# Four layers in one program: new planned costs, attention-value products by batch, and maxima laid between attention units

## The chip, the cores and the metric

The kernel runs on one core of a Trainium2 chip. The metric is the device time of one execution in microseconds. The engines are TensorE (PE, with its weight loads as PEld), VectorE (DVE), ScalarE (ACT), GpSimd (POOL) and SyncE (SP), which issues most transfers.

## The reference

The input x has 8 batches of 256 positions and 128 features; everything is float32. Four layers follow each other, each with a residual.

```python
x = x + moe0(x, cond)      # 2 shared blocks silu(x w1) * (x w3) w2, 8 experts gelu(x W1e) W2e, top 2 of 8
x = x + moe1(x, cond)      # 4 such shared blocks, 8 experts, top 2 of 8
# layer 2: a recurrence over the 256 positions
def step(h, z_t):
    gate = sigmoid(h @ Wh.T + z_t @ Wz.T + b)
    return tanh(h * (1 - alpha) + gate * z_t)
x = x + scan(step, h_t=cond, z=x)
# layer 3: causal attention, 16 heads of 8, with one more key and value made from cond
scores = q @ k.T / sqrt(8); causal; softmax; out = attn @ v; out @ c_proj_w + c_proj_b
x = x + attention(x, cond)
```

## The kernel before, in words

Positions are cut into 8 chunks of 32 (256 columns with the 8 batches). Both expert layers run chunk by chunk. The recurrence follows one chunk behind: step t is a product on TensorE (STEP, L1200), a tanh on ScalarE (GATE, L956), a scan on VectorE (SCAN, L1529) and a tanh on ScalarE (NEW, L961), with one small product on GpSimd (DECAY, L772). Each step needs the one before. All other work is laid between the steps. Behind some steps TensorE gets filler matmuls (L1204), so many that the planned work up to the next step reaches `DENSE` (0.62 us).

Attention works on 4 tiles t of 64 queries (`QT`). For each tile:
- KP and QP (L1053) project keys and queries, K and Q (L1060) spread them by groups of heads; QZ makes four copies of the queries, each masked to one head of a group, on VectorE (L1429) or, where `QZ_ACT` says so, on ScalarE (L912). V (L1067) makes the values, in two units of four batches.
- A (L1084, L1088) makes scores with the queries as rows, and VectorE takes each row's maximum (L1443). There are 1, 2, 4 and 4 such units a batch for t = 0 to 3. L and MT turn the maxima of a pair of batches p, with the image key's scores, into rows; SyncE writes these into QZ's copies (`rows_in`), so that the later scores come out less their maximum.
- S (L1132) makes scores with the keys as rows, for a batch b, half of the heads gg and block of 128 keys kb. On the diagonal block the causal term is added: for tiles in `CAUSAL_PE` by a further product on TensorE (L1137), for the others by VectorE (SC, L1496), which also moves the scores to SBUF. ScalarE takes the exponential (L947) into one of 8 buffers `pt`.
- AV (L1156) multiplies them with the values: 8 products of 32 output rows (16 records in the trace, as f32 goes in two), each in one of four column groups of the array. AC (L935) copies the sums out, X (L1112, L1116) transposes them and adds the image value's share, VectorE divides (L1479, L1484), TR and O (L1125, L1162) transpose back and project.

Tiles 0 and 1 have keys, queries and maxima made while the last two chunks' steps run (`EARLY`). The rest follows after the recurrence.

Nobody writes the order down. `plan` lists units with what they need, and `schedule` simulates the engines with the durations of `costs`: among the units that could start within `EAGER` us of the earliest, it takes the one listed first. `fits` keeps a unit out of the room before the next step, unless it ends in time, within `SLACK`. The resulting four lists are the program's order on each engine. No duration is used in any other way, apart from the number of fillers (`warming`). TensorE writes results into 4 banks of PSUM, 6 once the recurrence is over.

Of the kernel before, what the change touches and what calls it, by code (L numbers as in the profile page):

```python
# [24 lines left out]
ALU = mybir.AluOpType  # L25
# [92 lines left out]
def costs(key):  # L118

    k, c = key[0], key[1] if len(key) > 1 else 0  # L120
    if k == "W":
        a, b = PIECES[key[2]][1:]
        return {"act": (.18 + (b - a) * .00085,), "dve": (.16 + (b - a) * .00104,)}
# [28 lines left out]

# [10 lines left out]
def schedule(units):  # L163
# [15 lines left out]
    for key in chain + [u[0] for u in units]:  # L179
        family = (key[:3] if key[0] in ("R", "SA", "SB", "E", "M", "GT") else key if key[0] == "Y" else  # L180
                  key[0] if key[0] in ("STEP", "GATE", "SCAN", "NEW", "DECAY") else "P" if key[0] in ("KP", "QP") else key[:2])
# [25 lines left out]
    def start(key, part, eng):  # L207
# [17 lines left out]
        if eng == "pe":  # L225
            if key in banked:
# [18 lines left out]
        if eng == "act":  # L245
# [7 lines left out]
            if kind == "S" and s_users.index(key) >= NPT:  # L253
                av = (("AV",) + s_users[s_users.index(key) - NPT][1:], "pe")
# [53 lines left out]
    while queues:  # L308
        found = []
        for (eng, family), queue in queues.items():  # L310
            key, part = queue[0]
            at = start(key, part, eng)
            if at is not None and fits(key, eng, at, costs(key)[eng][part]):
                found.append((at, eng, number[key], family))
# [7 lines left out]
        if eng == "pe":  # L322
# [1289 lines left out]
```

## Time and profile before

| | |
|---|---|
| median of 3 runs | 479.9 us (478.22 to 479.98) |
| span of the profiled execution | 478.1 us |
| its share outside the span, by the median run | 1.8 us |
| TensorE, VectorE, ScalarE busy | 442.8, 309.3, 261.2 us |
| recurrence, first to last gate | 43.6 to 342.5 us |

The page of the profile gives its own execution's span; that execution's time outside the profiler is not known, so the median run stands beside it. Busy times add up what an engine worked on, whatever it cost the whole. The rows come after the change.

### The profile page before, as it was taken

To read this page: it belongs to the slowest core of one execution; us is meant where nothing else is said; L and a number is where in the kernel's file an instruction comes from. 1 tells how busy PE (TensorE), PEld (TensorE's weight loads), DVE (VectorE), ACT (ScalarE), POOL (GpSimd) and SP (SyncE) were. 2 spreads that over 40 slices of the span, in tenths; PEclk is the share of its full clock that TensorE was granted. 3 is DMA by queue.
4 is the path that set the end of the run, shared out by engine and by line. 5 is a ranking of instruction groups with operands and counts; after the bars stand their busy time and mean duration, and the time that the engine had idled before them with its cause. 6 is when DMAs were issued, how large, how long until landed. Compare 5 with 4: busy or idle time off the path is not lost.

```text
span 478.1 us, 13039 instructions
## 1 busy us (share of the span) xinstructions
PE 442.8 (93%) x4530; PEld 310.0 (65%) x4530; DVE 309.3 (65%) x999; ACT 261.2 (55%) x885; POOL 85.9 (18%) x365
## 2 busy tenths in 40 slices
PE   3999999899999999999998998999998798999984
PEld 2787787667777777776756766566655464656652
DVE  6774666666656556656557665576449978569851
ACT  3552646545646556456474356654777159764461
POOL 7120313221413213213121121211100000000000
PEclk9999999999999999999999999999999999999995
DMA  8400000000000000000000000000000001001000
GB/s 314 149 12 8 6 0 1 3 0 1 3 0 2 2 2 1 1 2 1 1 1 4 1 1 2 1 3 2 2 4 22 2 2 23 6 3 26 2 4 22
DMA packets 11222, 7.70 MB, mean 16 GB/s; under 512 B 8983, under 2 KB 10263, under 8 KB 11159
## 3 DMA queue, kind: packets, MB, share of 16 engines
q1 hardware_dynamic: 10727, 6.61, 4.5%
q8 instruction: 38, 0.62, 0.5%
q10 hardware_dynamic: 432, 0.27, 0.2%
q14 instruction: 25, 0.20, 0.1%
HBM read 5.39 MB, written 1.05 MB: 13 GB/s over the span
## 4 chain that ended last, share of the span: by engine, by line
PE 70%; ACT 13%; DVE 11%; issue 4%; DMA 1%; POOL 0%; ACTq 0%; DVEq 0%
PE ybk L1035 17%; PE cbk L1200 11%; PE hid L1180 7%; PE ybk L1156 6%; DVE cbk L1529 4%; ACT dd L956 4%; ACT hb L882 3%; DVE wm L1443 3%; ACT hs L961 2%; PE hid L1132 2%; PE vbk L1180 2%; PE hid L1084 2%; PE hid L1060 2%; PE hid L1053 1%; PE hid L1021 1%
## 5 line engine op out<-in xcount | busy, mean ns | idle before, releaser
L1529 DVE TENSOR_TENSOR_SCAN cbk<-dd 128x24 f32<-128x24 f32 x256 | 55.7, 218 | 102.3 <-ACT dd L956 98.9
L1200 PEld LDWEIGHTS cbk<-hs,rec 128*128 128x128 f32 x512 | 76.4, 188 | 56.2 <-ACT hs L961 49.1
L1200 PE MATMUL cbk<-hs,rec 128*128 128x8 f32 x512 | 91.5, 251 | 7.7 <-ACT hs L961 3.7
L772 POOL TENSOR_TENSOR dd<-hs,leak 128x8 f32<-128x8 f32 x256 | 55.1, 215 | 233.0 <-ACT hs L961 230.4
L1035 PE MATMUL ybk<-hg,down 128*128 128x256 f32 x352 | 95.8, 398 | 0.5 <-DVE hg L1405 0.2
L961 ACT ACTIVATE hs<-cbk 128x8 f32<-128x8 f32 x256 | 45.3, 177 | 70.5 <-DVE cbk L1529 69.2
L956 ACT ACTIVATE dd<-cbk 128x8 f32<-128x8 f32 x256 | 46.4, 181 | 61.6 <-PE cbk L1200 60.1
L1180 PE MATMUL hid<-xsp,up 128*128 128x256 f16 x528 | 73.1, 277 | 2.4 <-ACT hb L882 0.6
L1035 PEld LDWEIGHTS ybk<-hg,down 128*128 128x128 f32 x352 | 60.7, 191 | 6.3 <-DVE hg L1405 0.9
L1180 PEld LDWEIGHTS hid<-xsp,up 128*128 128x128 f16 x528 | 49.7, 105 | 10.9 <-ACT hb L882 2.9
L1156 PE MATMUL ybk<-hb,vx 128*32 128x64 f32 (+1 forms) x1536 | 38.2, 223 | 2.5 <-ACT hb L947 1.9
L1156 PEld LDWEIGHTS ybk<-hb,vx 128*32 128x32 f32 (+1 forms) x1536 | 25.5, 108 | 18.4 <-ACT hb L947 9.2
L947 ACT ACTIVATE hb<-hb 128x512 f32<-128x512 f32 (+1 forms) x48 | 29.2, 622 | 11.7 <-DVE hb L1496 8.7
L1405 DVE TENSOR_TENSOR hg<-hb,hid 128x512 f32<-128x512 f32 x49 | 32.9, 676 | 2.9 <-PE hid L1021 2.8
L882 ACT ACTIVATE hb<-hid 128x512 f32<-128x512 f32 x54 | 32.0, 593 | 2.6 <-PE hid L1180 2.0
L1443 DVE TENSOR_REDUCE wm<-hid 128x2 f32<-128x384 f32 (+3 forms) x49 | 29.6, 617 | 1.2 <-PE hid L1088 1.0
L1204 PE MATMUL cbk<-id 128*128 128x256 f16 x143 | 23.3, 270 | 0.0
L1496 DVE TENSOR_TENSOR hb<-hid,later 128x512 f32<-128x512 f32 (+1 forms) x27 | 18.0, 680 | 5.8 <-PE hid L1132 5.8
L1084 PE MATMUL hid<-kp,qz 128*128 128x128 f16 (+3 forms) x140 | 17.8, 233 | 3.3 <-DVE wm L1443 1.8
L1180 PE MATMUL vbk<-xsp,up 128*128 128x256 f16 x144 | 20.3, 278 | 0.2
L1132 PE MATMUL hid<-qz,kp 128*128 128x256 f16 (+1 forms) x102 | 19.5, 279 | 0.2 <-DVE wm L1443 0.2
L1021 PE MATMUL hid<-gt,sel 128*128 128x256 f16 x98 | 17.7, 273 | 0.2
(231 smaller groups left out, 661.0 us busy)
## 6 DMA issues: line engine op xcount, KB each, us to landing
qz<-up_in SPq DMA_DIRECT2D x3, 512.0 KB, 6.8
out_dram<-silu SPq DMA_DIRECT2D x4, 256.0 KB, 2.9
x<-x_in SPq DMA_DIRECT2D x7, 128.0 KB, 8.2
down<-down_in SPq DMA_DIRECT2D x1, 768.0 KB, 8.6
att<-att_in SPq DMA_DIRECT2D x1, 743.0 KB, 9.4
down<-down_in SPq DMA_DIRECT2D x1, 640.0 KB, 6.2
kp<-mrow SPq DMA_DIRECT2D x32, 4.0 KB
qz<-rows SPq DMA_DIRECT2D x32, 2.0 KB, 1.7
```

What stands on the lines that cost most here:

```text
L772: tts(dd[:, t % ZR, 1, :, 2], hs[:, t, :], leak[:, 0:1].broadcast_to([P, B]), ALU.mult).then_inc(decay, 1)
L882: nc.scalar.activation(hb[:, i % NHB, :], hid[bank_of[key]][:], ACT.Gelu, scale=1 / WS).then_inc(act_done, 1)
L947: nc.scalar.activation(pt[0:ks, i % NPT, :], scores, ACT.Exp, scale=SC).then_inc(act_done, 1)
L956: nc.scalar.activation(dd[:, t % ZR, 1, :, 0], cbk[c % 2][:, o:o + B], ACT.Tanh, scale=0.5).then_inc(gate_th, 1)
L961: nc.scalar.activation(hs[:, t + 1, :], new, ACT.Tanh).then_inc(h_full, 1)
L1035: m = pe.matmul(ybk[l][:, 0:n], D(l, "w2" if shared else "e2", e * f + i), hg[:, hg_of[made] % NHG, i * n:i * n + n], start=first and i == ...
L1156: m = pe.matmul(abk[i % 2][HP * j:HP * j + HP, g * P + QT * (b % 2):g * P + QT * (b % 2) + QT], vx[0:ks, kb, at:at + HP], w[:, (r * J + j) ...
L1180: m = pe.matmul(into, up[:, pw, a:a + P], x_part(c, l, px, slice(0, n)), start=j == 0, stop=j == 2)
L1200: pe.matmul(cbk[c % 2][:, o:o + B], wh, hs[:, t, :], start=False, stop=True, skip_group_check=True).then_inc(gate_pre, 1)
L1405: i = tts(hg[:, hg_of[key] % NHG, w], hb[:, hb_of["E", c, l, e] % NHB, w], hk[:, w], ALU.mult)
L1443: i = nc.vector.tensor_reduce(wm[:, t % 2, b, a * n + r.start:a * n + r.stop], hk[:, r.start * nk:r.stop * nk].rearrange("p (h k) -> p h k ...
L1529: nc.vector.tensor_tensor_scan(vps[chunk_of(t) % 2], dd[:, t % ZR, 0].rearrange("p b o -> p (b o)"), dd[:, t % ZR, 1].rearrange("p b o -> ...
```

## The change

- `costs` gets other durations, many of them shorter, and `schedule` counts a tail after a unit's end for each engine (`tail`) and a switch of the array's shape on TensorE (`switch`: 0.165 us into a narrower shape, 0.08 us out of it). `EAGER` goes from 0.1 to 0.03. At most two A units wait for VectorE (`MOST_A`). S, SC and AV each form one queue over all tiles.
- AV is one unit a batch: all 16 or 32 (for t = 2, 3) products with their second records follow each other.
- V is one unit a tile: four batches go to rows 0 to 63 of the bank, four to rows 64 to 127, alternating.
- `CAUSAL_PE` is (0, 1, 2): the addition on VectorE stays for t = 3 alone.
- `QZ_ACT` is empty: all of QZ is VectorE's.
- The maxima of a tile are listed between the attention units of the tile before, pair by pair; keys and queries of t = 3 come after the last pair of t = 1 (`KQ3 = 3`).

```diff
-QZ_ACT = ((), (), (0, 1, 2, 3), (0, 1, 2, 3))
+QZ_ACT = ((), (), (), ())
-EAGER = .1
+EAGER = .03
+MOST_A = 2
+KQ3 = 3
+INTO, OUT_OF = .165, .08
-CAUSAL_PE = (0,)
+CAUSAL_PE = (0, 1, 2)
...
     if k == "A":
-        return {"pe": ((.66, .38, .23, .28)[c],), "dve": (.69 if c != 2 else .55,)}
+        return {"pe": ((.66, .34, .23, .275)[c],), "dve": (.6 if c != 2 else .47,)}
     if k == "S":
-        return {"pe": (.43 if key[4] == c // 2 and not diagonal(key) else .22,), "act": (.6,)}
+        return {"pe": (.43 if key[4] == c // 2 and not diagonal(key) else .22,), "act": (.5,)}
     if k == "SC":
-        return {"dve": (.69,)}
+        return {"dve": (.6,)}
+    if k == "AV":
+        return {"pe": (.446 * (c // 2 + 1) + (INTO if c == 2 else 0),)}
...
-        "GT": {"pe": (.21,), "act": (.37,)}, "SA": {"pe": (.65,), "act": (.59,), "dve": (.69,)},
-        "SB": {"pe": (.65,), "dve": (.69,)}, "E": {"pe": (.65,), "act": (.59,)}, "M": {"pe": (.22,), "dve": (.69,)},
+        "GT": {"pe": (.13,), "act": (.27,)}, "SA": {"pe": (.655,), "act": (.5,), "dve": (.61,)},
+        "SB": {"pe": (.655,), "dve": (.61,)}, "E": {"pe": (.655,), "act": (.5,)}, "M": {"pe": (.22,), "dve": (.6,)},
...
-        "V": {"pe": (.48,), "dve": (.69,)}, "L": {"dve": (.2,)}, "MT": {"pe": (.55,), "act": (.25,), "dve": (.45,)},
-        "EI": {"act": (.25,)}, "AV": {"pe": (.4,)}, "AC": {"act": (.6,)}, "X": {"pe": (.85,), "dve": (.26, .29)},
+        "V": {"pe": (.44,), "dve": (.56, .56)}, "L": {"dve": (.15,)}, "MT": {"pe": (.25,), "act": (.17,), "dve": (.4,)},
+        "EI": {"act": (.2,)}, "AC": {"act": (.5,)}, "X": {"pe": (.84,), "dve": (.23, .24)},
...
+    tail = {"pe": .17, "act": .1, "dve": .08, "pool": 0.0}
...
+            if kind == "A" and sum(1 for k in users if k and k[0] == "A" and (k, "dve") not in end) >= MOST_A:
+                return None
...
+    def switch(key):
+
+        of = tiling(key)
+        if of == shape[0]:
+            return 0.0
+        return INTO if of != (P, P) else OUT_OF
...
+            if at is not None and eng == "pe" and not part and number[key] >= 0:
+                at = max(at, free["pe"] + switch(key))
...
-            end[key, eng] = free[eng] + (.17 if eng == "pe" else 0)
+            end[key, eng] = free[eng] + (tail[eng] if number[key] >= 0 or eng == "pe" else 0)
...
-    attend(0)
+    attend(0, *range(B // 2))
     keys_and_queries(2)
     for p in range(B // 2):
         maxima(2, p)
-    attend(1)
-    keys_and_queries(3)
-    maxima(3, 0)
-    attend(2)
-    attend(3, 1)
+        attend(1, p)
+        if p == KQ3:
+            keys_and_queries(3)
+    for p in range(B // 2):
+        maxima(3, p)
+        attend(2, p)
+    attend(3, *range(B // 2))
...
                 elif kind == "V":
-                    _, t, q = key
-                    r = slice(QT * (t % 2), QT * (t % 2) + QT)
+
+                    _, t = key
                     pe.wait_ge(dve_done, nth["dve", ("X3", t * QT + XP)])
                     for i in range(4):
-                        m = pe.matmul(hk[r, i * P:i * P + P], x3[:, 4 * q + i, t * QT:(t + 1) * QT], A("wv"),
-                                      start=True, stop=True)
+                        for q in range(2):
+                            m = pe.matmul(hk[QT * q:QT * q + QT, i * P:i * P + P], x3[:, 4 * q + i, t * QT:(t + 1) * QT],
+                                          A("wv"), start=True, stop=True)
...
+                    for kb in range(t // 2 + 1):
+                        ks = keys_of(t, kb)
+                        for gg in range(2):
+                            pe.wait_ge(act_done, nth["act", ("S", t, b, gg, kb)])
+                            w = pt[0:ks, s_order["S", t, b, gg, kb] % NPT, :]
```

## Rows read from the trace of the kernel before

**Rows 1.** The page, the span in 40 equal slices, in tenths

```profile
PE   3999999899999999999998998999998798999984
...
PEclk9999999999999999999999999999999999999995
```

**Rows 2.** The gate's line: durations in ns, first and last start

```profile
L956 ACT ACTIVATE dd<-cbk x256: 163/182/184, 43.6 to 342.5; 128x8 f32<-128x8 f32 x128
```

**Rows 3.** Timeline, three places in the recurrence: start, us, engine, line

```profile
271.46 0.31 PE L1200 MATMUL cbk<-hs,rec 128*128 128x8 f32 x2
...
272.58 0.31 PE L1200 MATMUL cbk<-hs,rec 128*128 128x8 f32 x2
...
291.20 1.28 ACT L927 ACT_TABLE_LOAD   x1
```

**Rows 4.** Stretches: length, busy us of PE, PEld, DVE, ACT, POOL, granted clock

```profile
43.00:342.00 299.00, 287.81 (x2263) 211.46 (x2261) 185.84 (x698) 163.45 (x695) 71.77 (x332) 1.00 0.01 2
342.00:359.00 17.00, 16.91 (x237) 9.80 (x236) 7.09 (x17) 13.20 (x26) 0.20 (x1) 1.00 0.04 10
359.00:385.00 26.00, 21.64 (x303) 12.79 (x302) 25.12 (x62) 11.55 (x25) 0.00 (x0) 1.00 0.04 8
...
434.00:455.00 21.00, 20.16 (x380) 12.82 (x378) 18.94 (x39) 10.55 (x22) 0.00 (x0) 1.00 0.07 16
455.00:466.00 11.00, 9.11 (x233) 5.59 (x231) 6.10 (x12) 8.05 (x17) 0.00 (x0) 1.00 0.02 5
```

**Rows 5.** Timeline: two operations of a kind in a row, VectorE and ScalarE

```profile
343.49 1.14 ACT L947 ACTIVATE hb<-hb 128x512 f32<-128x512 f32 x2
...
349.33 1.28 DVE L1496 TENSOR_TENSOR hb<-hid,later 128x512 f32<-128x512 f32 x2
...
357.42 0.62 DVE L1429 TENSOR_SCALAR qz<-fq,att 121x512 f16<-121x512 f16 x2 [0.31 <-ACT fq L903]
...
371.62 1.00 DVE L1443 TENSOR_REDUCE wm<-hid 128x2 f32<-128x384 f32 x2
```

**Rows 6.** Timeline of the weight loads, from 461.79 us

```profile
461.79 0.47 PEld L1112 LDWEIGHTS cbk<-small,hg 128*128 128x128 f32 x4
...
462.82 0.27 PEld L1156 LDWEIGHTS ybk<-hb,vx 128*32 128x32 f32 x16 [0.20 <-ACT hb L947]
463.18 0.11 PEld L1132 LDWEIGHTS vbk<-qz,kp 128*128 128x128 f16 x2
463.51 0.49 PEld L1156 LDWEIGHTS ybk<-hb,vx 128*32 128x32 f32 x32 [0.21 <-issue]
464.09 0.11 PEld L1132 LDWEIGHTS cbk<-qz,kp 128*128 128x128 f16 x2
```

**Rows 7.** Timeline: the causal product, and a unit of V

```profile
345.24 0.38 PE L1137 MATMUL hid<-ident,cz 128*64 128x512 bf16 x1
...
345.46 0.38 PE L1132 MATMUL vbk<-qz,kp 128*64 128x256 f16 x2
...
357.98 0.85 PEld L1067 LDWEIGHTS vbk<-att,x 128*64 128x64 f32 x8 [0.42 <-issue]
```

**Rows 8.** Groups by line from 342 us on: count, busy us, mean ns, idle before

```profile
L947 ACT ACTIVATE hb<-hb 128x512 f32<-128x512 f32 (+1 forms) x48 | 29.2, 622 | 11.7 <-DVE hb L1496 8.7 <-PE hid L1162 2.0 <-PE cbk L1132 0.4
...
L912 ACT ACTIVATE qz<-fq,att 121x512 f16<-121x512 f16 x16 | 10.7, 714 | 0.3
L947 ACT ACTIVATE hb<-hid 128x512 f32<-128x512 f32 (+1 forms) x17 | 9.8, 578 | 2.4 <-PE hid L1132 2.0 <-PE hid L1137 0.3
...
L1435 DVE TENSOR_TENSOR vx<-vbk,att 64x512 f32<-64x512 f32 x2 | 1.4, 689 | 1.1 <-PE vbk L1067 1.1
...
L1484 DVE TENSOR_TENSOR sel<-cbk,rden 128x128 f32<-128x128 f32 x6 | 1.8, 292 | 0.6
...
L1156 PE MATMUL ybk<-hb,vx 128*32 128x64 f32 (+1 forms) x1392 | 34.5, 224 | 2.3 <-ACT hb L947 1.7
```

**Rows 9.** The page, transfers: kind, count, KB each, us to landing

```profile
qz<-rows SPq DMA_DIRECT2D x32, 2.0 KB, 1.7
```

**Rows 10.** Stretches at the end, columns as in rows 4

```profile
466.00:472.00 6.00, 4.08 (x59) 2.36 (x60) 1.09 (x4) 1.56 (x3) 0.00 (x0) 0.69 0.00 0
472.00:478.00 6.00, 1.90 (x2) 0.33 (x2) 0.75 (x1) 0.00 (x0) 0.00 (x0) 0.50 0.19 44
```

More of the change, by code:

```diff
@@ L151, in costs, with tiling @@
     }[k]
+def tiling(key):
+    k = key[0]
+    if k == "S":
+        return (P, P) if keys_of(key[1], key[4]) == P else (P, QT)
+    if k == "AV":
+        return (P if key[1] else QT), HP
+    return (P, HP) if k in ("MT", "GT", "VI") else (P, QT) if k == "V" else (P, P)
 def landed(key):
@@ L180, in schedule @@
         family = (key[:3] if key[0] in ("R", "SA", "SB", "E", "M", "GT") else key if key[0] == "Y" else
[L181 removed]
+                  key[0] if key[0] in ("STEP", "GATE", "SCAN", "NEW", "DECAY") else "P" if key[0] in ("KP", "QP") else
+                  key[0] if key[0] in ("S", "SC", "AV") else key[:2])
         for eng, parts in costs(key).items():
@@ L336, in schedule @@
             if kind == "AV":
-                av_done[0] += 1
+                av_done[0] += 2 * (key[1] // 2 + 1)
         free[eng] = at + parts[part]
+        if eng == "pe":
+            shape[0] = (QT, QT) if kind == "X" else (QT, HP) if key[:2] == ("AV", 2) else tiling(key)
         lists[eng].append((key, part if len(parts) > 1 else None))
         if part == len(parts) - 1:
-            end[key, eng] = free[eng] + (.17 if eng == "pe" else 0)
+            end[key, eng] = free[eng] + (tail[eng] if number[key] >= 0 or eng == "pe" else 0)
             if number[key] >= 0:
@@ L395, in keys_and_queries @@
                             *([(("S", t - 2, B - 1, 1, (t - 2) // 2), "pe", eng)] if t >= 2 else []))
-        for i in range(2):
-            add(("V", t, i), True, ready)
+        add(("V", t), True, ready)
     def qz_engine(t, g, i, by):
@@ L413, in maxima, with attend @@
             (("E", NC - 1, 1, E * CHUNKS[-1] * B // 512 - 1), "act", "act"))
-    def attend(t, ahead=0):
-        for p in range(B // 2):
+    def attend(t, *pairs):
+        for p in pairs:
             i = t * B // 2 + p
-            if ahead and p + ahead < B // 2:
-                maxima(t, p + ahead)
             for b in (2 * p, 2 * p + 1):
@@ L427, in attend @@
                             add(("SC", t, b, gg, kb), False, (("S", t, b, gg, kb), "pe", "dve"))
-                        add(("AV", t, b, gg, kb), False, (("S", t, b, gg, kb), "act", "pe"),
-                            *[(("V", t2, 1), "dve", "pe") for t2 in range(t + 1)],
-                            *([(("AC", *divmod(i - 2, B // 2)), "act", "pe")] if (b % 2, gg, kb) == (0, 0, 0) and i >= 2 else []))
-            add(("AC", t, p), False, (("AV", t, 2 * p + 1, 1, t // 2), "pe", "act"),
+                add(("AV", t, b), False, *[(("S", t, b, gg, kb), "act", "pe") for gg in range(2) for kb in range(t // 2 + 1)],
+                    *[(("V", t2), "dve", "pe") for t2 in range(t + 1)],
+                    *([(("AC", *divmod(i - 2, B // 2)), "act", "pe")] if b % 2 == 0 and i >= 2 else []))
+            add(("AC", t, p), False, (("AV", t, 2 * p + 1), "pe", "act"),
                 *([(("X", *divmod(i - 2, B // 2)), "pe", "act")] if i >= 2 else []))
@@ L437, in attend @@
                     *([(("O", t - 2), "pe", "dve")] if t >= 2 else []))
-        add(("O", t), True, *[(("TR", t, u), "dve", "pe") for u in range(2)])
+            if p == B // 2 - 1:
+                add(("O", t), True, *[(("TR", t, u), "dve", "pe") for u in range(2)])
     mm4 = lambda n: 4 * n / 2.4
@@ L1430, in unit @@
                 elif kind == "V":
-                    _, t, q = key
-                    r = slice(0, 4)
-                    n = slice(QT * (t % 2), QT * (t % 2) + QT)
+                    _, t = key
+                    n, m = slice(QT * (t % 2), QT * (t % 2) + QT), slice(QT * part, QT * part + QT)
                     dve.wait_ge(pool_set, 4)
-                    i = tts(v_of[n, t // 2, 4 * q + r.start:4 * q + r.stop, :, 0:HD],
-                            hk[n, :].rearrange("p (b h d) -> p b h d", b=4, h=H)[:, r],
-                            A("vb")[n].rearrange("p (o h d) -> p o h d", o=1, h=H).broadcast_to([QT, r.stop - r.start, H, HD]),
-                            ALU.add)
+                    i = tts(v_of[n, t // 2, 4 * part:4 * part + 4, :, 0:HD], hk[m, :].rearrange("p (b h d) -> p b h d", b=4, h=H),
+                            A("vb")[m].rearrange("p (o h d) -> p o h d", o=1, h=H).broadcast_to([QT, 4, H, HD]), ALU.add)
                 elif kind == "A":
```

59 lines of the change are left out of this document (28 added, 31 removed).

## The prediction

> **What bounds the kernel now.** I read the page first. TensorE is busy in nearly every slice and its granted clock is full up to the last slices [rows 1]. That busy share says little: a matmul counts from its start to its modelled end, so short matmuls with small holes between them look like full work. So I cut the execution into two parts by the recurrence. Its gate activation runs 256 times, the first at 43.6 us, the last at 342.5 us [rows 2]. That is 298.9 us for 255 intervals, 1.172 us each. Where the chain is undisturbed, one step follows another after 1.12 us [rows 3], as from 271.46 to 272.58, so the chain cannot be below 255 x 1.12 = 285.6 us, and 13 us of it are slips. Some are other work in the way: a table load of 1.28 us on ScalarE sits inside one step [rows 3].
>
> The other part, 342.5 to 478.1 us, is 135.6 us of attention with no chain. The stretches [rows 4] show what limits it. From 359 to 385 VectorE is busy 25.12 of 26 us: 32 maxima of the third tile (t=2) run there, 0.46 us apart [rows 5], while TensorE needs about 0.22 us for each. There it is VectorE. In 342:359 and 434:455 TensorE is busy 99 and 96%. After 455 it waits for exponentials, and the last matmul is followed only by the eviction and the store.
>
> **Prices on TensorE**, from the weight-load queue in order of start [rows 6]. One attention-value (AV) unit, 16 loads at 462.82, takes 0.36 us to the next score; two units at 463.51 take 0.58. So a further unit costs 0.22. From the score at 463.18 to the next AV are 0.33. The product with the causal matrix, 512 columns, spaces the next matmul by 0.22 (345.24 to 345.46) [rows 7], and a score pair has 2 x 256 columns, so 0.22 too. A run of AV between scores thus costs 0.36 + 0.33 - 0.22 - 0.22 = 0.25 us above its first unit and the score. By columns, a maxima unit of t=2 (2 x 192 + 128) is 0.22, one of t=3 (2 x 256 + 128) 0.27, a K or Q piece (2 x 512) 0.44. An X unit takes 1.03 from 461.79 to the AV behind it, 0.9 without the entry into AV. V's eight f32 records of 128 columns take 0.9 (0.85 of loads and the rest of the last one [rows 7]); KP, QP and O stream as many f32 columns in two records, 0.9 too. An MT unit has ten short records; I take 0.4, above one AV run's 0.36.
>
> **The change, part by part.**
>
> AV by batch. After 342 us the load queue has 59 separate runs of AV, for 1392 loads [rows 8] or 87 units; with one run per batch and tile, t=1 to 3 have 24, and some 3 are left of t=0. (59 - 27) x 0.25 = 8.0 us of TensorE goes. The units stay.
>
> Causal product for t=1 and t=2. VectorE loses 32 additions, 0.61 apart (1.28 for two) [rows 5]: 19.5 us. TensorE gets 32 products of 0.22: 7.0 us. ScalarE's exponentials read PSUM (578 ns) instead of SBUF (622 ns) [rows 8]. A score no longer waits for an addition before its exponential.
>
> QZ. 16 scalings of 714 ns leave ScalarE (11 us) [rows 8] and become 16 more on VectorE at 0.28 apart (0.62 for two [rows 5]): +4.5 us. Net VectorE is 15 us lighter, nearly all of it after 342.
>
> V. Eight matmul records of 128 columns take 0.9 us in one half of the array [rows 7]. The change gives each half eight. If the halves work at once, a tile costs 0.9 where it costs 1.8; AV shows such an overlap, 16 records of 64 columns in 0.22 us where eight of 128, in one half, take 0.9. If not, nothing is saved. Three of the eight old units run after 342, so 1.3 us there, between 0 and 1.3; those before sit between chain steps. The evictions stay. The Trainium skill, TensorEngine Tiling (Array Packing), section "PSUM Bottleneck", says that tiling speeds up TensorE but not the emptying of PSUM. Two evictions of about 0.69 us per tile are there in the trace of before as well [rows 8]; by that rule V's 1.3 us would be worth nothing where VectorE is the limit.
>
> Maxima between attention units. It adds no work. It puts t=2's maxima (VectorE 0.46, TensorE 0.22 each) beside t=1's attention, and t=3's beside t=2's; now t=3's maxima run beside t=3's own attention up to 455. SyncE's small row transfers move along with MT, still a whole tile ahead of the scores that wait for them, so I cost them at nothing; if that cover were gone, one transfer of 1.7 us [rows 9] would stand in front of the first score of each of three tiles, 5 us.
>
> The planner's durations. The old plan charged VectorE 0.69 for operations that start 0.61 apart, ScalarE 0.6 for 0.52, AV 0.4 whether switched or not, MT 0.55. The new ones are close to the starts in the trace, V (0.44) excepted, which stays too low by 0.45. This moves the order everywhere and is the least certain part.
>
> **The sum, after 342 us**, by what each stage asks of TensorE and VectorE:
> - rest of t=0, keys and queries of t=2: 17 us now, 16 after (two or three AV runs, half a V).
> - t=1 with maxima of t=2. TensorE: 16 scores 3.5, causal 3.5, AV 3.5, 8 runs 2.0, 32 maxima 7.0, 4 X 3.6, 4 MT 1.6, transposes and output 1.5: 26.2. VectorE: maxima 14.7, QZ 4.5, small operations of four pairs 5.2, output 1.6: 26.0. (The small ones are estimates: a pair of batches has five no longer than the division's 0.29 [rows 8], 1.3 us; two transposes' copies and the output's sum are of the size of an addition of 512 columns or half of it.) I take 28.
> - keys and queries of t=3: 2 x 0.9 + 8 x 0.44 + 0.9 = 6.2; I take 7.
> - t=2 with maxima of t=3. TensorE: 7.0 + 3.5 + 7.0 + 2.0 + 8.6 + 3.6 + 1.6 + 1.5 = 34.8; VectorE 19.5 + 5.2 + 1.6 = 26.3. I take 36.
> - t=3 alone. TensorE: 7.0 + 7.0 + 2.0 + 3.6 + 0.6 = 20.2. ScalarE: 32 exponentials and 4 copies at 0.52 (1.14 for two [rows 5]) 18.7. I take 23.
> - from the last AV to the end 12.1 us now; 11 after.
>
> This makes 121 us. By the same prices the old kernel asks TensorE for 16 + 26.2 + 6.2 + 34.8 + 20.2 - 7.0 + 8.0 + 1.3 = 105.7, plus 12.1 of drain, so 18 of its 135.6 us are waits. After the change the same sum is 103.4 + 11 = 114.4, and 121 would leave 6.6. With three engines within 10 to 20% of each other in two stages I don't believe that; I leave 9, so 123.5: a gain of 12 us. Of the 13 us of slips in the chain I give back 2, between -5 (more operations squeezed into a step) and +8. Total 14 us.
>
> The profiled span is 478.1 us, the median run 479.9, so 1.8 us lies outside the span. 478.1 - 14 + 1.8 = 465.9; I say 466.
>
> **Rivals.**
> - *The waits stay (0.15).* On TensorE alone the change is 8.0 + 1.3 - 7.0 = 2.3 us. If the starvation of 359:385 only moves (the maxima still come in a lump, since the planner takes what can start first), little more than that, the shorter drain and 1 to 2 us of VectorE comes out: 475. For it: in that stage VectorE with QZ added is still 26.0 by my sum. Against: there TensorE now does little else, and afterwards the other work lies beside it.
> - *TensorE's clock falls in t=3 (0.10).* With no maxima beside it, the last tile alternates between TensorE (20.2) and ScalarE (18.7). In the old trace the granted clock fell to 0.69, then 0.5, the 1.2 GHz level, after 455:466, where TensorE waited for exponentials [rows 10]. At that level from the middle of the stage, 10 us of work costs 10 more, partly hidden by ScalarE: 8 of the 14 us go, 474. The Trainium skill, TensorE: Matmul & The Clock Gate, section "Why this matters for your kernels", says that idle gaps between bursts take TensorE back to its low clock; the trace agrees in those last stretches and shows no fall in 359:385.
> - *Slower: the chain slips more (0.08).* With smaller costs the planner puts two VectorE operations into one step: 0.60 + 0.33 beside the scan's 0.22 is 1.15, over 1.12. This turns the forecast into no gain when the mean step, 1.172 now, grows by the 12 us of the attention part, 12/255 = 0.047 us, to 1.219; at 1.25 the time is 479.9 - 12 + 20 = 488. Against: VectorE is busy 185.84 of 299 us there [rows 4], so it need not crowd.
> - *More than forecast (0.12).* The chain's slips halve (6 us) and the waits fall to 5 (114.4 + 5 = 119.4, 16 less than 135.6): 458, and with 8 us out of the chain 456.
> - *My forecast (0.55)*, its own range 460 to 472.
>
> From these: faster by over 0.5% (below 477.5), which is about what a measurement of this kernel can tell from no change: 0.55 + 0.12, 0.10 of the waits' 0.15 and 0.06 of the clock's 0.10, together 0.83. Within 0.5%: 0.05 and 0.02 of those two, 0.07. Slower: 0.08 and the last 0.02 of the clock's, 0.10. The range, 456 to 477, reaches to the better case at one end and takes in the clock and most of the waits at the other.
>
> **What would show it.** The load queue after 342 with about 27 AV runs of 32 or 64 loads. 16 causal additions on VectorE in place of 48. No qz on ScalarE. VectorE busy after 342 lower by about 15 us, and TensorE's idle less than 10 us outside the drain. Last gate near 340. V's 16 records within about 1 us. I am wrong if the last gate comes after 350, if TensorE waits for maxima as long as now, or if the clock leaves 1.00 before the last tile's last pair.

## The result, and the profile after

The changed kernel takes 448.8 us (median of 4 runs, 447.85 to 449.41), against 479.9 (4 runs, 478.22 to 481.19): ratio 0.935, 95% interval 0.933 to 0.937. That is 31 us faster where I forecast 14, and below my range of 456 to 477. The profiled span is 446.1 us, of an execution of 447.85 us: 1.8 us lie outside it, as before, and it is 1.0 us below the median. Times here are medians of fast executions; two of before_eager's five ran some 9 us slower at a lower granted clock (0.970 instead of 0.990 to 0.994) and are left out.

The page's slices of the changed kernel, in tenths, as in [rows 1]:

```profile
PE   3999999999999999999999999899999999999994
DVE  5875665776566575665665877357734988993562
PEclk9999999999999999999999999999999999999998
```

The gate and the AV loads by line: durations in ns, then first and last start in us.

```profile
L987 ACT ACTIVATE dd<-cbk x256: 164/182/184, 42.7 to 341.0; 128x8 f32<-128x8 f32 x128
L1188 PEld LDWEIGHTS ybk<-hb,vx x1536: 102/110/113, 301.4 to 437.0; 128*32 128x32 f32 x128, 64*32 64x32 f32 x64
```

The last gate starts at 341.0, before at 342.5 [rows 2]; the chain itself is 298.3 us long, before 298.9. So all but 1.5 us of the gain lies behind the last gate. What follows it, which I call the tail, takes 105.0 us instead of 135.6. The stretches from there on, columns as in [rows 4]:

```profile
341.00:352.00 11.00, 11.00 (x220) 8.40 (x219) 10.09 (x29) 6.74 (x15) 0.00 (x0) 1.00 0.01 4
352.00:364.00 12.00, 12.00 (x163) 8.86 (x165) 11.56 (x28) 6.58 (x13) 0.00 (x0) 1.00 0.11 25
364.00:376.00 12.00, 11.90 (x217) 8.36 (x205) 9.92 (x30) 7.58 (x18) 0.00 (x0) 1.00 0.01 3
376.00:388.00 12.00, 11.73 (x196) 7.43 (x195) 11.26 (x29) 6.01 (x13) 0.00 (x0) 1.00 0.11 25
388.00:400.00 12.00, 12.00 (x225) 8.47 (x223) 11.83 (x26) 5.32 (x12) 0.00 (x0) 1.00 0.02 4
400.00:412.00 12.00, 12.00 (x224) 7.26 (x220) 4.71 (x14) 8.22 (x18) 0.00 (x0) 1.00 0.02 4
412.00:424.00 12.00, 11.99 (x311) 8.66 (x308) 6.70 (x13) 9.40 (x18) 0.00 (x0) 1.00 0.02 6
424.00:435.00 11.00, 10.72 (x311) 8.24 (x311) 7.35 (x15) 9.42 (x19) 0.00 (x0) 1.00 0.12 26
435.00:446.00 11.00, 4.95 (x144) 3.07 (x142) 2.31 (x7) 2.27 (x5) 0.00 (x0) 0.85 0.11 25
```

The reader is to see two things. TensorE (second number) fills each stretch up to 435: the stretch like 359:385 of [rows 4], where it was busy 21.64 of 26 us, is gone. And VectorE is busy 9.9 to 11.8 of each 11 or 12 us up to 400, so the maxima run beside the attention without holding TensorE. Between the last gate and the start of the last AV load TensorE is busy 95.3 us, before 114.8, and idle 0.7, before 9.9. VectorE is busy 75.7 us in the tail, before 93.4.

The groups by line from 341 us on, to be laid beside [rows 8]:

```profile
L1188 PE MATMUL ybk<-hb,vx 128*32 128x64 f32 (+1 forms) x1312 | 23.5, 220 | 0.0
...
L978 ACT ACTIVATE hb<-hid 128x512 f32<-128x512 f32 (+1 forms) x31 | 17.8, 585 | 7.9 <-PE hid L1169 7.4 <-PE hid L1164 0.3
...
L1461 DVE TENSOR_SCALAR qz<-fq,att 121x512 f16<-121x512 f16 x32 | 8.8, 345 | 1.2 <-ACT fq L934 0.9 <-PE cbk L1169 0.3
```

1312 of 1536 AV matmul records, each with one weight load, are left after the gate: 224, or 14 units of 16, were done among the steps, before 9. ScalarE's exponentials now wait for TensorE, the sign of a TensorE that is the limit. Where each stage of my sum ended:

| | forecast | measured |
|---|---|---|
| last gate to the first maxima of t=2 (before 17.1) | 16 | 4.4 (341.0 to 345.4) |
| t=1, maxima of t=2, keys and queries of t=3 | 35 | 30.3 (to 375.7) |
| t=2, maxima of t=3, t=3, up to the last AV | 59 | 61.3 (to 437.0) |
| last AV to the end | 11 | 9.1 |
| packing allowance | 2.5 | – |

The first stage holds 11.6 of the 18.5 us by which the tail came out shorter. The border is not clean: after 345.4 two AV units of t=0 and its output still follow, and some scores of t=1 come before it. A weight-load count tells more. Ahead of the last gate went 48 K and Q loads instead of 32, 12 of KP and QP instead of 8, 224 of AV instead of 144, and 11 of X instead of 4, while the chain got no longer. The keys and queries of t=2, which I had after the gate, are all among the steps.

### The profile page after: what moved, and what is told of

Its sections match the earlier page's. It is cut to its first block, busy times and chain, and to the rows that moved or that the text cites. A ratio compares the mean times of both kernels' runs of the same rounds, so it can differ in the third digit from the quotient of the medians.

```text
span 446.1 us, 13036 instructions
## 1 busy us (share of the span) xinstructions
PE 422.6 (95%) x4553; PEld 305.4 (68%) x4553; DVE 290.1 (65%) x983; ACT 249.5 (56%) x869; POOL 86.9 (19%) x365
## 4 chain that ended last, share of the span: by engine, by line
PE 72%; ACT 13%; DVE 9%; issue 3%; DMA 1%; POOL 1%; ACTq 0%; DVEq 0%
PE ybk L1066 17%; PE cbk L1232 12%; PE hid L1212 7%; PE ybk L1188 5%; DVE cbk L1558 4%; ACT dd L987 3%; PE hid L1164 3%; PE hid L1116 2%; ACT hs L992 2%; PE vbk L1212 2%; ACT hb L913 2%; PE hid L1052 2%; PE cbk L1164 2%; ACT hb L978 1%; PE hid L1084 1%
## 5 line engine op out<-in xcount | busy, mean ns | idle before, releaser
L1232 PE MATMUL cbk<-hs,rec 128*128 128x8 f32 x512 | 93.9, 256 | 5.4 <-ACT hs L992 1.7
L1212 PE MATMUL hid<-xsp,up 128*128 128x256 f16 x504 | 68.9, 275 | 0.3 <-DVE lg L1376 0.3
L1472 DVE TENSOR_REDUCE wm<-hid 128x2 f32<-128x512 f32 (+3 forms) x50 | 31.2, 638 | 2.5 <-PE hid L1120 2.5
L978 ACT ACTIVATE hb<-hid 64x512 f32<-64x512 f32 (+1 forms) x43 | 24.8, 585 | 7.9 <-PE hid L1169 7.4
L1188 PE MATMUL ybk<-hb,vx 128*32 128x64 f32 (+1 forms) x1536 | 28.0, 220 | 0.0
L1212 PE MATMUL vbk<-xsp,up 128*128 128x256 f16 x168 | 23.5, 277 | 0.0
L1236 PE MATMUL cbk<-id 128*128 128x256 f16 x134 | 20.9, 271 | 0.0
L1461 DVE TENSOR_SCALAR qz<-fq,att 121x512 f16<-121x512 f16 x64 | 18.2, 343 | 1.2 <-ACT fq L934 0.9
L1116 PE MATMUL hid<-kp,qz 128*128 128x64 f16 (+3 forms) x164 | 17.4, 226 | 1.0 <-issue 0.2
L1212 PEld LDWEIGHTS vbk<-xsp,up 128*128 128x128 f16 x168 | 16.5, 108 | 2.0
```

The costliest lines, as they stand in the source:

```text
L1188: m = pe.matmul(abk[i % 2][HP * j:HP * j + HP, g * P + QT * (b % 2):g * P + QT * (b % 2) + QT], vx[0:ks, kb, at:at + HP], w[:, (r * J + j) ...
L1212: m = pe.matmul(into, up[:, pw, a:a + P], x_part(c, l, px, slice(0, n)), start=j == 0, stop=j == 2)
L1232: pe.matmul(cbk[c % 2][:, o:o + B], wh, hs[:, t, :], start=False, stop=True, skip_group_check=True).then_inc(gate_pre, 1)
L1472: i = nc.vector.tensor_reduce(wm[:, t % 2, b, a * n + r.start:a * n + r.stop], hk[:, r.start * nk:r.stop * nk].rearrange("p (h k) -> p h k ...
```

## The experiments

Two theories stood against each other. *Work:* the parts save TensorE what they save (switches, halves of V) and VectorE its additions, each for itself. *Room:* the time follows how much attention the plan gets into the room between the steps, and the parts matter because their units fit there, or lie so that none waits. "Ahead" is the count of AV units (16 loads) ahead of the last gate, "gate" the start of the last gate, "tail" the time from it to the end.

| kernel | us | ratio to before, 95% | ahead | gate | tail | AV runs in the tail |
|---|---|---|---|---|---|---|
| before | 479.9 | 1 | 9 | 342.5 | 135.6 | 59 |
| after | 448.8 | 0.935 (0.933 to 0.937) | 14 | 341.0 | 105.0 | 19 |
| costs_alone | 467.1 | 0.976 (0.972 to 0.980) | 5 | 341.0 | 124.8 | 41 |
| u_costs | 465.7 | 0.974 (0.971 to 0.976) | 6.75 | 340.3 | 122.9 | 26 |
| old_but_av | 465.0 | 0.971 (0.967 to 0.975) | 10 | 341.9 | 119.9 | 24 |
| undo_av | 453.2 | 0.946 (0.941 to 0.951) | 13 | 341.5 | 110.0 | 32 |
| undo_causal | 460.7 | 0.961 (0.956 to 0.966) | 14 | 341.1 | 117.2 | 24 |
| undo_qz | 453.4 | 0.945 (0.941 to 0.950) | 14 | 341.1 | 109.2 | 19 |
| undo_v | 455.3 | 0.949 (0.944 to 0.954) | 10.75 | 342.0 | 111.4 | 22 |
| u_list | 450.7 | 0.941 (0.940 to 0.943) | 14 | 342.3 | 107.2 | 19 |
| late_kq | 450.6 | 0.943 (0.940 to 0.947) | 16 | 341.5 | 106.8 | 20 |
| old_table | 450.8 | 0.940 (0.938 to 0.943) | 16 | 347.2 | 101.8 | 18 |
| no_switch | 449.5 | 0.937 (0.935 to 0.938) | 16 | 344.1 | 103.9 | 23 |
| eager | 461.3 | 0.962 (0.959 to 0.965) | 6 | 344.3 | 115.5 | 21 |
| eager_08 | 453.7 | 0.946 (0.941 to 0.951) | 12 | 344.7 | 106.8 | 22 |
| eager_0 | 454.4 | 0.947 (0.945 to 0.948) | 8 | 341.5 | 111.8 | 20 |
| most_a | 456.8 | 0.951 (0.947 to 0.956) | 10 | 340.4 | 113.6 | 23 |
| v_price | 460.8 | 0.961 (0.959 to 0.964) | 0 | 338.2 | 120.5 | 21 |
| v_fits | 447.7 | 0.933 (0.932 to 0.935) | 14 | 340.5 | 104.7 | 20 |
| before_eager | 477.8 | 0.996 (0.994 to 0.998) | 13 | 344.9 | 132.6 | 64 |

**The planner alone, and all but the planner.** costs_alone has the new durations, tails, switch, `EAGER`, `MOST_A` and queues on the old AV, V, causal term, QZ and listing; u_costs is the reverse.

```diff
+++ costs_alone, against the changed kernel
-QZ_ACT = ((), (), (), ())
+QZ_ACT = ((), (), (0, 1, 2, 3), (0, 1, 2, 3))
-CAUSAL_PE = (0, 1, 2)
+CAUSAL_PE = (0,)
-        return {"pe": (.446 * (c // 2 + 1) + (INTO if c == 2 else 0),)}
+        return {"pe": (.223,)}
...
+++ u_costs (and the old durations), against the changed kernel
-EAGER = .03
-MOST_A = 2
+EAGER = .1
+MOST_A = 9
-INTO, OUT_OF = .165, .08
+INTO, OUT_OF = 0.0, 0.0
-    tail = {"pe": .17, "act": .1, "dve": .08, "pool": 0.0}
+    tail = {"pe": .17, "act": 0.0, "dve": 0.0, "pool": 0.0}
```

> The new durations, tails, switch times, EAGER, MOST_A and the joined queues of S, SC and AV are there; AV by unit, V in two units, causal term and QZ as before, and the units listed as before. Theory A (the durations carry much of the gain, since they pull the keys and queries of t=2 in among the recurrence's steps and fill holes afterwards): 464 to 472 us, last gate still near 341, fewer than 32 loads of K and Q pieces after it. Theory B (the gain is AV's switches, VectorE's additions and the lump of maxima, which the durations leave as they are): 476 to 481 us, AV still in 50 runs or more after the last gate, and the stretch in which VectorE makes t=2's maxima as full as before.

> The changed kernel with the old durations (AV and V charged with the old price of their units together), no tails, no switch times, EAGER 0.1 and no limit on A. Theory A: 460 us or more, since what the durations gave is lost. Theory B: at most 453 us.

Each is faster than before by 2.4 to 2.7%, and together they give 6.5%: 467.1 and 465.7 are gains of 12.8 and 14.3 us, 27.1 in sum, 4 less than the 31.1 of both (7 less by the ratios). Both times fit the range of theory A, but its reason, the durations, does not hold up below (old_table). Neither gets more AV ahead: 5 and 6.75 units, fewer than before. costs_alone does have the keys and queries of t=2 among the steps (48 and 12 loads, as the changed kernel), 5.3 us at my prices, but ten score pairs, five causal products, four AV units and half a tile of V fewer than before, 5.1 us by the same prices. So a net amount of work ahead appears only with both.

**One part undone.** undo_av goes back to AV by unit, undo_v to two units of V a tile, undo_causal and undo_qz to the old constants above.

```diff
+++ undo_av
-                add(("AV", t, b), False, *[(("S", t, b, gg, kb), "act", "pe") for gg in range(2) for kb in range(t // 2 + 1)],
+                        add(("AV", t, b, gg, kb), False, (("S", t, b, gg, kb), "act", "pe"),
...
+++ undo_v
-        add(("V", t), True, ready)
+        for i in range(2):
+            add(("V", t, i), True, ready)
```

> The changed kernel with AV planned and issued by unit (16 records), each unit free to go as soon as its own exponentials are there; the switch times stay in the plan. Theory A (after the change TensorE is the limit and a part is worth its TensorE time): AV in 40 to 60 runs after the last gate instead of 19, each more 0.25 us, so 5 to 10 us: 454 to 459. Theory B (the planner, now knowing the price of a switch, keeps units together by itself): at most 451.

> The changed kernel with the causal term of t=1 and 2 added by VectorE again. Theory A (TensorE is the limit and VectorE has room): the 7.0 us of products go, 442 to 445 us. Theory B (VectorE becomes the limit beside the maxima: 75.7 of 105 us busy after the last gate now, 95 with the additions, and it is 90% busy in the two stages with maxima already): 455 to 460 us.

> The changed kernel with half of QZ for t=2 and 3 on ScalarE again (16 of 0.66 us against 16 of 0.28 on VectorE). Theory A: TensorE's work is the same, 448 to 450. Theory B (VectorE, 4.5 us lighter, was the limit between 376 and 400 us): 445 to 447. Theory C (the longer scalings delay t=3's first maxima, for which everything there waits): 451 to 455.

> The changed kernel with V in two units of one half of the array each. If the two halves work at once: two tiles after the last gate cost 0.9 us more each, 450 to 452 us, and the 16 records of a tile in the changed kernel's trace span about 1 us against 1.8 here. If they don't, no difference, 448 to 449.5.

undo_av costs 4.4 us for 13 more runs; at my 0.25 us that is 3.3. The time falls between the ranges of both theories, since there are 32 runs and not 40 to 60; one AV unit and two K and Q loads fewer stand ahead. The trace still shows the hole of entering AV (last column: idle before, by its cause). Timeline of the weight loads of the changed kernel:

```profile
424.61 0.94 PEld L1188 LDWEIGHTS ybk<-hb,vx 128*32 128x32 f32 x64 [0.20 <-issue]
425.64 0.11 PEld L1164 LDWEIGHTS cbk<-qz,kp 128*128 128x128 f16 x2
...
426.62 0.94 PEld L1188 LDWEIGHTS ybk<-hb,vx 128*32 128x32 f32 x64 [0.21 <-issue]
427.65 0.11 PEld L1164 LDWEIGHTS hid<-qz,kp 128*128 128x128 f16 x2
```

A run is now 64 loads, a whole batch, with one hole of 0.20 to 0.21 us. The Trainium skill, TensorEngine Tiling (Array Packing), section "Key Properties", says that a change of the tiling mode drains TensorE; the trace agrees with these holes of 0.20 and 0.21 us.

undo_causal costs 11.9 us, the dearest part. Its stretches after the gate, and its waits (us in total, times, longest):

```profile
341.00:352.00 11.00, 8.51 (x106) 6.53 (x105) 10.06 (x29) 4.26 (x10) 0.00 (x0) 0.81 0.01 1
352.00:364.00 12.00, 10.95 (x167) 6.88 (x165) 10.46 (x25) 3.58 (x7) 0.00 (x0) 0.89 0.11 24
364.00:376.00 12.00, 10.38 (x181) 6.60 (x181) 11.83 (x29) 5.68 (x13) 0.00 (x0) 1.00 0.02 4
...
388.00:400.00 12.00, 9.91 (x161) 5.91 (x162) 11.69 (x28) 4.23 (x8) 0.00 (x0) 0.86 0.11 25
```

```profile
ACT hb L978 <- DVE hb L1525: 19.0, 15, 4.6
...
PEld hid L1116 <- DVE wm L1472: 3.6, 6, 2.3
```

Here VectorE is the limit: the exponentials wait 19.0 us for additions, up to 4.6 at once. TensorE is idle 9.3 us up to the last AV instead of 0.7, and its granted clock reads 0.81, 0.89 and 0.86 in three stretches. VectorE's 94.9 us in the tail stand against 75.7. The 7 us of products that TensorE is spared are less than what it then waits. Narrower stretches show that 0.81 and 0.89 are one fall, across the border at 352:

```profile
341.00:347.00 6.00, 5.21 (x88) 4.13 (x87) 5.17 (x20) 3.03 (x8) 0.00 (x0) 1.00 0.01 3
347.00:355.00 8.00, 6.29 (x58) 4.58 (x59) 7.00 (x15) 1.86 (x3) 0.00 (x0) 0.57 0.01 2
355.00:364.00 9.00, 7.95 (x127) 4.70 (x124) 8.35 (x20) 2.95 (x6) 0.00 (x0) 1.00 0.14 31
```

The missing share of the clock, times the length of its stretch, is 2.1 + 1.3 + 1.7 = 5.1 us. By this estimate the low clock takes at most 5.1 of the 11.9 us, since part of it fell in waits.

undo_qz costs 4.6 us, though it takes 4.5 us of scalings off VectorE (16 x 0.28; VectorE is busy 72.5 us in the tail instead of 75.7). Timeline of ScalarE:

```profile
378.96 2.54 ACT L943 ACTIVATE qz<-fq,att 121x512 f16<-121x512 f16 x4
```

Four scalings in a row, 2.54 us, stand in front of the exponentials. Up to the last AV TensorE is idle 1.9 us more and busy 1.3 us more, and the rest comes 0.9 us later. That the scalings cause all of it is not shown.

undo_v costs 6.5 us. V's weight loads after the last gate, first in the changed kernel, then in undo_v, and then V's matmuls over the whole of undo_v:

```profile
342.35 1.11 PEld L1099 LDWEIGHTS cbk<-att,x 128*64 128x64 f32 x16
343.33 1.01 PEld L1099 LDWEIGHTS hid<-att,x 128*64 128x64 f32 x16
```

```profile
347.75 1.01 PEld L1099 LDWEIGHTS cbk<-att,x 128*64 128x64 f32 x8
348.73 1.40 PEld L1099 LDWEIGHTS hid<-att,x 128*64 128x64 f32 x16
350.10 0.90 PEld L1099 LDWEIGHTS vbk<-att,x 128*64 128x64 f32 x8
```

```profile
L1099 PE MATMUL hid<-att,x 128*64 128x128 f32 x40 | 4.8, 278 | 0.0
...
L1099 PE MATMUL vbk<-att,x 128*64 128x128 f32 x16 | 2.1, 276 | 0.0
...
L1099 PE MATMUL cbk<-att,x 128*64 128x128 f32 x8 | 1.0, 272 | 0.0
```

The two halves do work at once: 16 records take 0.98 us from start to start (342.35 to 343.33), as long as the first eight of undo_v (347.75 to 348.73). The sum over the kernel is 7.9 us in undo_v and 4.8 in the changed kernel, 3.1 less. After the last gate it is four old units in 3.3 us against two new ones in 2.0, so 1.3 us, as forecast; the other 1.8 lie among the steps. The rest goes with the room: undo_v has 10.75 units ahead instead of 14, 6 K and Q loads fewer, and a last gate at 342.0. Its plan also charges V 0.44 for each of two units, twice the changed kernel's price for a tile, and the run cannot tell this from the halves.

**Listing, and one block of work moved.** u_list lists the units in the old order. late_kq lets KP and QP of t=2 start only after the last step:

```diff
+++ late_kq
+        after = [(("NEW", T - 1), "act", "pe")] if t == 2 else []
-            add((kind + "P", t), True, ready, (("VI", 1), "dve", "act"),
+            add((kind + "P", t), True, ready, *after, (("VI", 1), "dve", "act"),
```

> The changed kernel with the units listed as before: all maxima of t=2 ahead of t=1's attention, those of t=3 one pair ahead within t=3. If the list is what takes the starvation away: the maxima of t=2 come in a lump again, TensorE waits for them 8 us or more, 457 to 464 us. If the planner fills those holes by itself once AV and the additions no longer stand in the way: at most 452 us.

> The changed kernel, with the projections of keys and queries of t=2 held back until the recurrence is over, nothing else changed. If moving them among the steps is worth what they cost on TensorE (2 x 0.9 + 8 x 0.44 = 5.3 us) and the wait for the first scores of t=2 is hidden: 453 to 456 us. If other work of the attention takes their room among the steps: 448 to 451. If the attention after the recurrence hangs on them: above 457.

The listing is worth 1.9 us, and late_kq loses 1.8, not the 5.3 us that it takes out of the room: scores (46 loads instead of 28), causal products (23 instead of 14) and AV (16 units) took the place. So it isn't the keys that matter, but that the room is filled with something.

**Which number of the planner.** eager, eager_08 and eager_0 set `EAGER` to 0.1, 0.08 and 0; most_a sets `MOST_A` to 9; no_switch plans switches as free; old_table has the old durations but for AV and V, and no tails on ScalarE and VectorE; old_but_av is u_costs with AV at the trace's price and V at 0.48 us instead of 0.96.

```diff
+++ eager
-EAGER = .03
+EAGER = .1
+++ most_a
-MOST_A = 2
+MOST_A = 9
+++ no_switch
-        if of == shape[0]:
+        if True:
+++ old_table
-        return {"act": (.08 + (b - a) * .00085,), "dve": (.16 + (b - a) * .00104,)}
+        return {"act": (.18 + (b - a) * .00085,), "dve": (.16 + (b - a) * .00104,)}
...
-        return {"pe": (.43 if key[4] == c // 2 and not diagonal(key) else .22,), "act": (.5,)}
+        return {"pe": (.43 if key[4] == c // 2 and not diagonal(key) else .22,), "act": (.6,)}
```

> The changed kernel with EAGER at 0.1 again, nothing else. If taking the next unit strictly by when it can start is what packs TensorE: fewer attention units among the recurrence's steps and idle TensorE after it, 452 us or more. If only the durations count: 448 to 450.

> The changed kernel with EAGER 0.08. Its plan has the first AV before step 226 and 6 AV units ahead of the last step; EAGER 0.03 has step 223 and 7 units (448.8 us), EAGER 0 step 227 and 4 units (454.4), EAGER 0.1 step 242 and 3 units (461.3). If the time follows how much of the attention stands ahead of the last gate: 450 to 454 us, below that of EAGER 0. If it rises with EAGER by itself: 457 or more.

> The changed kernel with EAGER 0. If a smaller EAGER packs better throughout: at most 449 us. If 0.03 is one good order among scattered ones (in this plan 4 AV units stand ahead of the last step, in the changed kernel's 7): 452 us or more.

> The changed kernel without the limit of two A units that wait for VectorE. If the limit keeps banks free for the others: the plan has 5 AV units ahead of the last step instead of 7 and K and Q pieces of t=2 behind it, 451 to 455 us. If the banks were free anyway: 448 to 450.

> The changed kernel with switches of the array's shape free in the plan (AV's own price for t=2 stays). If knowing them matters: more switches after the last gate and steps that slip where a unit of another shape ends later than planned, 452 us or more. If AV's batches have taken the switches out already: 448 to 451.

> The changed kernel with the old durations of all units but AV and V, and without the tails of ScalarE and VectorE; switch times, EAGER and MOST_A stay new. If the durations are what lets more units into the steps' gaps: the keys and queries of t=2 fall behind the last gate again, 457 us or more. If the switch times and EAGER are what counted: at most 453.

> The kernel of u_costs (all planning as before the change) with one price changed: AV at 0.446 us a pair of units and 0.25 once a run, where it charged 0.8 a pair; V at 0.48. If u_costs lost 17 us mostly because a wrong price of AV's batches misplaced what stands beside them: 454 us or less. If all the durations share in it: 460 to 466.

The durations, which I had called the least certain part, are worth 2.0 us, and the planned switch 0.7, which the intervals do not tell from nothing. In old_table the recurrence starts later, with its first gate at 48.0 instead of 42.7 us, and the tail is 3.2 us shorter. old_but_av, 465.0 us as against 465.7, shows that u_costs did not lose by a wrong price of AV. `EAGER` at 0.1 costs 12.5 us, at 0.08 4.9 and at 0 5.6; `MOST_A` at 9 costs 8.0. In eager the first AV comes late and few come ahead (the AV line, as above):

```profile
L1188 PEld LDWEIGHTS ybk<-hb,vx x1536: 102/110/113, 328.7 to 449.6; 128*32 128x32 f32 x128, 64*32 64x32 f32 x64
```

That `EAGER` helps by itself is refuted by the kernel before with that number (its S, SC and AV joined into one queue each over the tiles, as in the change):

```diff
+++ before_eager
-EAGER = .1
+EAGER = .03
-                  key[0] if key[0] in ("STEP", "GATE", "SCAN", "NEW", "DECAY") else "P" if key[0] in ("KP", "QP") else key[:2])
+                  key[0] if key[0] in ("STEP", "GATE", "SCAN", "NEW", "DECAY") else "P" if key[0] in ("KP", "QP") else
+                  key[0] if key[0] in ("S", "SC", "AV") else key[:2])
```

> The kernel before, with EAGER 0.03 and one queue each for S, SC and AV (with a queue a tile the plan gets stuck at this EAGER: scores of t=1 take all eight buffers), old durations. If EAGER alone packs TensorE: 465 to 470 us, as much as the 12.5 us that it gave in the changed kernel. If it only helps where AV's batches and the lighter VectorE leave holes to fill: 475 or more.

477.8 us: with 13 units ahead, but 64 AV runs and 9.7 us of idle TensorE in the tail. The tail is 3.0 us shorter and the last gate 2.4 us later, so nearly nothing is left. VectorE is busy 93.5 us of the tail, as before; that it is VectorE which keeps more room from paying here is my reading, and no run shows it.

**The room alone.** The cleanest cut is V's planned price. The change says 0.44 where the trace has 0.98. In v_price it says 0.9: such a unit doesn't fit before the next step. In v_fits the plan charges 0.9 all the same, and only the question whether it fits goes by 0.44. Apart from the number of fillers, both kernels run the instructions of the changed kernel in another order.

```diff
+++ v_price
-        "V": {"pe": (.44,), "dve": (.56, .56)}, "L": {"dve": (.15,)}, "MT": {"pe": (.25,), "act": (.17,), "dve": (.4,)},
+        "V": {"pe": (.9,), "dve": (.56, .56)}, "L": {"dve": (.15,)}, "MT": {"pe": (.25,), "act": (.17,), "dve": (.4,)},
+++ v_fits, that and
+        if key[0] == "V" and eng == "pe":
+            cost = .44
```

> The changed kernel with V planned at 0.9 us, about what its 16 records take in the trace (1.0), in place of 0.44. If the wrong price makes steps slip where V lies among them: 446.5 to 448. If V is too rare for it (four units): no difference, 448 to 449.5.

> The kernel of v_price, with V planned at 0.9 us, but let into the room between two steps as if it took 0.44, as in the changed kernel. If v_price lost 12 us because its V found no room before the last gate and all of t=0's AV stood behind it: 447 to 450, with 12 AV units or more ahead of the last gate. If planning V at its real length is what hurts: above 455.

Gate, AV and V by line of v_price:

```profile
L987 ACT ACTIVATE dd<-cbk x256: 163/182/184, 42.5 to 338.2; 128x8 f32<-128x8 f32 x128
...
L1188 PEld LDWEIGHTS ybk<-hb,vx x1536: 102/110/113, 343.7 to 448.6; 128*32 128x32 f32 x128, 64*32 64x32 f32 x64
...
L1099 PEld LDWEIGHTS hid<-att,x x48: 132/137/137, 338.1 to 341.5; 128*64 128x64 f32 x48
```

and of v_fits:

```profile
L990 ACT ACTIVATE dd<-cbk x256: 163/182/185, 42.6 to 340.5; 128x8 f32<-128x8 f32 x128
...
L1191 PEld LDWEIGHTS ybk<-hb,vx x1536: 102/110/113, 299.8 to 436.2; 128*32 128x32 f32 x128, 64*32 64x32 f32 x64
...
L1102 PEld LDWEIGHTS hid<-att,x x32: 132/137/137, 154.6 to 204.6; 128*64 128x64 f32 x32
```

With V's true price all but 4 of its 64 loads wait for the end of the recurrence, and as AV needs the values, no AV unit is ahead. The last gate comes 2.8 us earlier (338.2), the tail is 15.5 longer, the kernel 12 us slower than the changed one, which is outside both of my ranges. Of the 15.5 us TensorE is busy for 11.3 and idle for 3.0 up to the last AV, and what follows takes 1.1 more. What fills the room instead are filler matmuls; their loads in v_price, then in the changed kernel:

```profile
L1236 PEld LDWEIGHTS cbk<-id x190: 95/96/181, 51.1 to 337.4; 128*128 128x128 f16 x190
```

```profile
L1236 PEld LDWEIGHTS cbk<-id x134: 95/96/181, 51.4 to 339.6; 128*128 128x128 f16 x134
```

v_fits, which tells the two uses of the number apart, takes 447.7 us, with an interval that overlaps the changed kernel's. It is the fastest kernel here, but not measurably faster.

## Why the prediction was wrong

The direction, and each part's sign on its engine, were right. None of the three signs that I had named for being wrong came, and the signs that I had named for being right did, but for 19 AV runs instead of 27. Two terms of the sum failed. The first is its first stage, "rest of t=0, keys and queries of t=2: 17 us now, 16 after": I took a tail with a fixed list of work and put what could move ahead of the last gate at nothing, where some 7 us moved. The second is the waits, of which I wrote "I leave 9", where 1.5 are left. My own terms close the account; the loads are counted in the traces, but their prices are the prediction's, so these are estimates.

- *Work that went ahead of the gate, which I had as 0:* KP and QP of t=2 2 x 0.9, eight K and Q pieces 3.5, five AV units 1.1, 7 of an X unit's 8 loads 0.8, three more causal products of t=0 0.7, less two score pairs (0.4) and half a tile of V (0.6): 6.9 us.
- *Waits, 9 forecast.* The TensorE sum was 103.4; less these 6.9 and 2.0 for the eight further AV runs that went (19 instead of 27) it is 94.5. TensorE was busy 95.3 and idle 0.7 up to the last AV: 1.5 us of waits. 7.5 us. This is a remainder and takes in every error of a price: for the kernel before the same sum leaves 18 where the profile has 9.9 us of idle time. What the other 8 were is open.
- *AV runs:* the 2.0 us just named. The end, from the last AV on, 9.1 instead of 11: 1.9. Here I had cut the kernel before at 466.0; its last AV load starts at 467.2, so the 12.1 us of my sum were 10.9.

Together 18.3 of the 18.5 us between 123.5 and 105.0. Against them the last gate came at 341.0, not 340.5, and the median run is 1.0 us above the profiled one: 17 us, the miss.

By the steps, in order:
- *AV by batch* was right in kind, 0.25 us a run; undoing it gives 4.4 for 13 runs. The runs came to 19, since runs of two batches join (the last one has 128 loads, 435.24 to 437.09).
- *Causal product:* right in its counts, undersized in effect. I priced a VectorE 15 us lighter (it was 17.7) and let it show only where VectorE was the limit. Undone, it costs 11.9 us: TensorE is idle 9.3 us instead of 0.7, and at a low clock for a part.
- *QZ* I counted as a cost to VectorE and no gain; undoing it costs 4.6 us. On ScalarE it stands in front of exponentials, which I take for the cause; it is not shown.
- *V:* the overlap of the halves was right (0.98 against 0.9), and so, in size, were the 1.3 us after the gate; the worth was not: 6.5 when undone. The rule of the Trainium skill on emptying PSUM (TensorEngine Tiling (Array Packing), section "PSUM Bottleneck"), by which it would be worth nothing where VectorE is the limit, did not decide: the tail has TensorE idle for 0.7 us only.
- *Maxima between attention units:* the listing alone is worth 1.9. `MOST_A` is worth 8.0, with 10 units ahead instead of 14 when undone; whether it works through the banks or by keeping maxima apart, no run tells. The fall of the clock in t=3 did not come: the granted clock stays 1.00 up to 435.
- *Durations:* I noted that V's price "stays too low by 0.45" as a blemish. It is what lets V and then AV in among the steps: 12 us (v_price against v_fits and the changed kernel).
- *Chain:* 2 us given back forecast, 0.6 measured. None of the rivals came; the nearest, more than forecast, had the waits at 5 and halved slips, down to 456 us, and neither it nor I had moved work.

Undoing single planning numbers and parts, one at a time (nine runs), costs 52 us in all where the change brings 31. So the parts are not terms of a sum; that each needs the others to keep all engines fed is my reading of it. Room explains the trend of the tails (16 or 14 units ahead: 101.8 to 107.2 us in six kernels; 6 or 0 ahead: 115.5 and 120.5), but not undo_causal and undo_qz, which have the same loads ahead as the changed kernel and tails of 117.2 and 109.2. In undo_causal the limit is VectorE. And a shorter tail is not all: in old_table, no_switch and eager_08 the last gate comes 3 to 6 us later.

Open: how much of undo_causal's 11.9 us is the clock, within the 5.1 us, and how much the waits; and why the plan's choice at `EAGER` 0.1 leaves the attention of t=0 so late. I can say that it does, not what in the list rule brings it about.

## What to carry to other kernels

When an order comes from a planner, count what each stage asks of each engine, and then ask what can move over the stage's edge: free room beside a chain of steps that wait for each other (filler matmuls show it) can be worth as much as a faster instruction. One kind of unit that is too long for the room kept everything that depends on it out of it here, and made the tail 15 us longer. And undo parts one by one before crediting them: here their single worths add up to far more than the whole.

## What I had not expected of the hardware

- In undo_causal the granted clock was 1.00 in 341:347, where TensorE was busy 5.21 of 6 us, and 0.57 in the next 8 us, most of them at the 1.2 GHz level, while the kernel before kept 1.00 over 26 us with 21.64 busy [rows 4]. What makes the difference no run here shows.
- 16 f32 V records in two column halves took 0.98 us from start to start, and eight in one half took 0.98 as well (undo_v).
